# Graph network kernel: early banks at product tiles 10 to 31, five of six copied ahead, banks 17 and 23 copied by VectorE

## The reference, cut to what matters

```python
msg = x[src] + edge_attr                                # 206,250 edges of 128 numbers
agg = segment_sum(msg, dst, num_segments=6250)          # edges are sorted by dst
h = relu(agg @ W1 + b1) @ W2 + b2
# then a norm over everything, a norm per column, gelu, two residuals and a layer norm
```

## Time and profile before

| what | value |
|---|---|
| median of 3 runs | 779.25 us (778.49 to 780.11) |
| the profiled execution's own time | 778.32 us |
| its span, first to last instruction | 776.5 us |
| PE busy | 688.2 us, 89% |
| DVE busy | 619.9 us, 80% |
| ACT busy | 445.7 us, 57% |
| first product of chunk 0, of chunk 24 | 83.48 us, 667.46 us |

### The profile page before, as it was taken

How to read it: one execution, slowest core, us unless ns; L and a number is a source line. 1 busy time by engine, 2 the same in 40 slices (tenths; PEclk the granted TensorE clock), 3 DMA queues, 4 the chain that set the end, 5 groups by cost and what they waited for, 6 DMA issues and landing times.

```text
span 776.5 us, 25426 instructions
## 1 busy us (share of the span) xinstructions
PE 688.2 (89%) x9447; PEld 624.4 (80%) x9447; DVE 619.9 (80%) x1049; ACT 445.7 (57%) x993; POOL 101.2 (13%) x68
## 2 busy tenths in 40 slices
PE   1975999999999999999999999999999999989650
PEld 1954988998889988899888998889988899868530
DVE  5787898888988889888898888988888888435684
ACT  1934467655676556765567655676556765325475
POOL 2143110111101111011110112101111011000000
PEclk9986999999999999999999999999999999999965
DMA  7867466255662566525665256652565535350006
GB/s 175 288 215 218 138 208 198 64 189 195 205 194 67 185 199 203 187 75 180 204 202 172 92 176 209 196 183 87 176 209 191 178 97 176 106 160 6 0 0 165
DMA packets 88984, 123.60 MB, mean 159 GB/s; under 512 B 8572, under 2 KB 84446, under 8 KB 88763
## 3 DMA queue, kind: packets, MB, share of 16 engines
q1 hardware_dynamic: 82220, 116.30, 47.0%
q0 software_dynamic: 5744, 5.38, 2.6%
q10 hardware_dynamic: 1000, 1.65, 0.8%
HBM read 119.23 MB, written 4.03 MB: 159 GB/s over the span
## 4 chain that ended last, share of the span: by engine, by line
PE 65%; DVE 13%; issue 8%; ACT 6%; DVEq 4%; DMA 3%; ACTq 0%; SPq 0%; POOLq 0%
PE bank L792 39%; PE bank L758 10%; DVE pool_m L1079 8%; PE bank L709 5%; ACT counts L583 4%; PE bank L842 3%; PE bank L852 3%; PE bank L681 3%; DVEq L1006 2%; PE bank L723 1%; DMA edges<-in_edge_attr_dram 1%; DMA agg<-in_dst_dram 1%; ACT pool_m L665 1%; DVE onehot L990 1%; DMA begins<-listed,tile_slot 1%
## 5 line engine op out<-in xcount | busy, mean ns | idle before, releaser
L583 ACT CAST counts<-bank 128x490 fp32r<-128x490 f32 x625 | 329.3, 593 | 237.1 <-PE bank L758 222.8
L792 PE MATMUL bank<-counts,x_hi 128*128 128x250 f32 x1225 | 309.0, 291 | 12.1 <-ACT counts L583 12.1
L792 PE MATMUL bank<-counts,x_lo 128*128 128x250 f32 x1225 | 293.1, 279 | 0.0
L1079 DVE TENSOR_TENSOR pool_m<-value_row,turned_lo 128x3328 bf16<-128x3328 bf16 (+1 forms) x125 | 229.3, 1835 | 64.8 <-PE bank L758 64.6
L792 PEld LDWEIGHTS bank<-counts,x_hi 128*128 128x128 f32 x1225 | 231.2, 189 | 17.8 <-ACT counts L583 17.8
L792 PEld LDWEIGHTS bank<-counts,x_lo 128*128 128x128 f32 x1225 | 231.8, 189 | 0.0
L758 PE MATMUL bank<-pool_m 128*128 128x98 bf16 x3125 | 199.2, 211 | 15.6 <-DVE pool_m L1079 15.6
L758 PEld LDWEIGHTS bank<-pool_m 128*128 128x128 bf16 x3125 | 159.2, 99 | 37.1 <-issue 16.3
L1079 DVE TENSOR_TENSOR pool_m<-value_row,turned_key 128x2548 bf16<-128x2548 bf16 (+1 forms) x125 | 179.8, 1439 | 0.0
L709 PE MATMUL bank<-edges,onehot 128*32 128x128 f32 x3228 | 121.1, 284 | 4.5 <-DMA edges<-in_edge_attr_dram 3.7
L476 POOL DMA_INDIRECT near<-listed,row_slot x27 | 53.6, 1986 | 512.2 <-DVE row_slot L1041 469.6
(11 more groups left out here) (153 smaller groups left out, 420.5 us busy)
## 6 DMA issues: line engine op xcount, KB each, us to landing
edges<-in_edge_attr_dram SPq DMA_DIRECT2D x134, 768.0 KB, 8.2
out_dram<-pool_m SPq DMA_DIRECT2D x6, 512.0 KB
agg<-in_dst_dram SPq DMA_DIRECT2D x1, 768.0 KB
agg<-in_src_dram ACTq DMA_DIRECT2D x1, 768.0 KB
listed<-agg ACTq DMA_DIRECT2D x1, 768.0 KB
begins<-listed,tile_slot POOLq DMA_INDIRECT x28, 4.1
near<-listed,row_slot POOLq DMA_INDIRECT x27
pool_m<-in_L_gnn_W_dram SPq DMA_DIRECT2D x2, 128.0 KB, 2.8
```

The source lines that it names most:

```text
L583: nc.scalar.copy(counts[:, :, at:at + NODES], cps[k % RING][:, 0:NODES * NT].rearrange("p (n q) -> p q n", q=NT)).then_inc(banks_free, 1)
L792: last = nc.tensor.matmul(sps[:, 0:CHUNK], part[:, q, :], counts[:, q, at:at + CHUNK], start=(q == 0 and part is x_hi), stop=(q == NT - 1 ...
L1079: last = dve.tensor_tensor(to[b % MARKED][:, 0:wide[1]], values[:, :, 0:n, :].to_broadcast(wide), of.to_broadcast(wide), ALU.is_equal)
```

## The change

The six banks of the next chunk are still counted during the products, now under the name `COUNTED = 6`, but at tiles 10, 14, 18, 22, 26 and 31 in place of 22, 27, 32, 37, 42 and 47. Only five of them are copied during the products (`AHEAD = 5`, so 50 more columns in place of 60); the sixth stays in PSUM until `chunk_summed` and becomes the first copy of the counting phase. Of the 25 copies of each chunk, those of banks 17 and 23 move from ScalarE to VectorE (`keep_bank`, same source, destination and size), with a semaphore of their own, `banks_kept`, that TensorE waits for before it uses their ring places again and before the products. The VectorE order gets `keep_bank(c, 17)` behind `mark_batch(c, 4)`, and `keep_bank(c, 23)` ahead of `mark_batch(c + 1, 0)`.

```diff
-AHEAD = 6
-AHEAD_AT = (22, 27, 32, 37, 42, 47)
+AHEAD = 5
+COUNTED = 6
+COUNTED_AT = (10, 14, 18, 22, 26, 31)
+KEPT = (17, 23)
...
                 act.wait_ge(chunk_summed, c + 1)
                 for k in range(AHEAD, BANKS):
-                    copy_bank(c, k, odd)
+                    if k not in KEPT:
+                        copy_bank(c, k, odd)
...
                 if k >= RING:
-                    pe.wait_ge(banks_free, c * BANKS + (k + 1 - RING))
+                    if k - RING in KEPT:
+                        pe.wait_ge(banks_kept, c * len(KEPT) + (KEPT.index(k - RING) + 1))
+                    else:
+                        pe.wait_ge(banks_free, c * (BANKS - len(KEPT)) + (k + 1 - RING - sum(j < k - RING for j in KEPT)))
...
-                for k in range(AHEAD, BANKS):
+                for k in range(COUNTED, BANKS):
                     count_bank(c, k)
...
-                pe.wait_ge(banks_free, (c + 1) * BANKS)
+                pe.wait_ge(banks_free, (c + 1) * (BANKS - len(KEPT)))
+                pe.wait_ge(banks_kept, (c + 1) * len(KEPT))
...
-                    if q in AHEAD_AT and more:
-                        count_bank(c + 1, AHEAD_AT.index(q))
+                    if q in COUNTED_AT and more:
+                        count_bank(c + 1, COUNTED_AT.index(q))
...
+            def keep_bank(c, k):
+
+                dve.wait_ge(chunk_summed, c + 1)
+                dve.wait_ge(banks_done, c * BANKS + (k + 1 + CREDIT))
+                dve.tensor_copy(counts[:, :, k * NODES:(k + 1) * NODES],
+                                cps[k % RING][:, 0:NODES * NT].rearrange("p (n q) -> p q n", q=NT)
+                                ).then_inc(banks_kept, 1)
...
@@ -1138,6 +1154,7 @@
                 put(first)
                 mark_pair(p, 3)
                 mark_batch(c, 4)
+                keep_bank(c, KEPT[0])
                 if not last:
                     mark_pair(p, 4)
                     split_words(c + 2)
...
                     mark_pair(p, 5)
                     mark_pair(p, 6)
+                keep_bank(c, KEPT[-1])
+                if not last:
                     mark_batch(c + 1, 0)
...
                 mark_pair(p, 8)
                 mark_batch(c, 4)
+                keep_bank(c, KEPT[0])
                 add(first + 2, 0, base_of(first + 2), c + 1)
                 put(first + 3)
                 mark_pair(p, 9)
...
                 put(first + 4)
                 mark_pair(p + 1, 0)
+                keep_bank(c, KEPT[-1])
                 mark_batch(c + 1, 0)
```

More of the change, by code:

```diff
@@ L110, in gnn_kernel @@
     AHEAD_N = AHEAD * NODES
-    assert AHEAD * BANK <= EDGES_OF[2] and EDGES_OF[-1] == PAIRS + 1
+    assert AHEAD <= COUNTED and COUNTED * BANK <= EDGES_OF[2] and EDGES_OF[-1] == PAIRS + 1
     SPAN = 2 * P
@@ L292, in gnn_kernel @@
         banks_free = sem("banks_free")
+        banks_kept = sem("banks_kept")
         chunk_summed = sem("chunk_summed")
@@ L796, in _ @@
             pe.wait_ge(x_split, NT // PIECE)
-            for k in range(AHEAD):
+            for k in range(COUNTED):
                 count_bank(0, k)
```

## The result

The changed kernel takes 781.46 us (median of 8 runs, 780.27 to 783.73); the kernel before, measured again beside it, 778.96 us. The ratio is 1.0033, 95% interval 1.002 to 1.0046. It is 0.33% slower. The forecast was 774.3 us, with a range of 769.5 to 778.6 us and 0.76 on faster and 0.11 on slower; the time lies above the range.

What follows compares the result with a forecast made beforehand. TensorE was taken to bound the kernel, with reachable waits in each pair of chunks. Pairs gain 4.1 us and the last counting phase 0.8, together about 4.9 us, giving 774.3 us for a median, range 769.5 to 778.6 us.

Steps and rivals of the forecast that it cites:

- Part 1: ScalarE ends its counting-phase copies about 0.7 us sooner; first product about 10.15 us (odd), 10.25 us (even) after phase start.
- Part 2: Each bank copy on VectorE: a row of 0.667 us, costing the engine 0.58 us.
- B: Rival: the VectorE copy takes its engine more than 0.68 us; at 0.85 us the kernel takes 787 us; chance 0.11.
- C: Rival: the VectorE copy costs 0.667 us without overlap; 778.4 us, no change; chance 0.13 together with the rest of D.
- Part 3: VectorE's counting phase: after bank 17's copy and small operations, marks of batch 0 start 9.87 us (odd), 9.66 us (even) in.
- the register load: VectorE, odd chunks: loading the address `base_of`, some 0.65 us in all, fits behind bank 17's copy.
- Part 4: TensorE in the products: stands at tile 10 for the marks of batch 0, about 0.6 us (odd) and 0.5 us (even).
- 2.5 us of room: TensorE at tile 22 in the kernel before: some 2.5 us to spare there.
- The sum: Whole kernel: 11.5 pairs of chunks at 0.36 us give -4.1 us, last counting phase -0.8 us; about -4.9 us, 774.3 us.
- the old wait at bank 20: TensorE in odd counting phases of the kernel before: waits 0.19 us for marks of batch 4, which the change removes.
- D: Rival: ScalarE's last copy or VectorE's dispatch costs 0.1 to 0.2 us more a chunk; 0.07 still faster, rest within C's 0.13.

Runs made afterwards that it cites:

- run 1: Changed kernel with bank 17's VectorE copy moved behind add(first + 2) and put(first + 3) in odd chunks: 770.91 us, ratio 0.9898 to the kernel before.
- run 4: Changed kernel with early banks still at tiles 10 to 31, but all 25 copies on ScalarE: 777.0 us, ratio 0.9974 to the kernel before.
- run 8: Changed kernel with the first VectorE copy behind add and put in odd chunks, and bank 15 in place of 17: 769.9 us, ratio 0.9894.
- run 7: Changed kernel with bank 17's copy behind add and put in odd chunks, and early banks at tiles 14 to 34: 762.96 us, ratio 0.9801.
- run 2: Changed kernel with only the address load of add(first + 2) moved ahead of bank 17's copy in odd chunks: 776.6 us, ratio 0.9971.
- run 3: Changed kernel with the two VectorE copies kept, but early banks at tiles 22 to 47 and six copied ahead: 778.14 us, ratio 0.9998.
- run 6: Changed kernel with early banks at tiles 14 to 34 in place of 10 to 31, VectorE order kept: 773.15 us, ratio 0.9924.

## Why the prediction was wrong

**Part 1, ScalarE's end and the first product.** The numbers are right: in even chunks C' + 10.25, measured 278.15 - 267.90 = 10.25. In odd chunks the same number was hidden by the missed wait, and appeared when that was removed (run 1: 10.14 for 10.15). The hit is in part luck. ScalarE's last copies in the changed kernel:

```profile
276.76 1.15 ACT L586 CAST counts<-bank 128x490 fp32r<-128x490 f32 x2
```

They end at 277.91, C' + 10.01, where before they ended at C' + 10.84: 0.83 us sooner, and not 0.7. But the first product now starts 0.24 us behind them, and before it started 0.05 us behind (251.77 + 1.99 = 253.76, product at 253.81). I had no term for that step of 0.19 us. In the changed kernel it is there in 24 of the 25 chunks and absent in the last, whose code stands behind the loop; in run 4, without the copies on VectorE and without TensorE's wait for `banks_kept`, it is absent in all. VectorE's own last copy is not what is late: in run 8 it ends 1.19 us ahead of the product (273.53, 274.72), and the product still starts 0.24 us behind ScalarE (274.48). What is left is the wait for `banks_kept`, one wait more between the one for ScalarE's copies and the first product in TensorE's queue (`chunk_added` stands there in both kernels); no run has moved that wait by itself, so this cause is argued. In the changed kernel the stall at tile 10 hides the step. In run 7 nothing does, and 24 times 0.19 us is an estimate of 4.6 us at most that is still to be had there.

**Part 2, the price of the copy.** Right. 0.66 to 0.67 us a row, 0.667 forecast; the next instruction starts 0.58 us after the copy's start (253.03 to 253.61), 0.58 forecast. Rivals B and C fall with this. By the drain rule of the Trainium skill ("VectorE: DVE Perf Modes", section "The DRAIN you can't avoid") the slot would have been the whole 0.66 us. The same section makes an exception, which the forecast left out: a next instruction that is not held starts earlier. The 0.58 us of this trace go with the exception and not with the rule.

**Part 3, the small operations behind bank 17.** This is the step that failed: "The operations ahead of it are done at about 6.82 + 1.33 = 8.15". I followed VectorE's queue to VectorE's own next wait, the turn at bank 20, and found room. I did not ask who on another engine waits for the operations in between. The first of them is `add(first + 2)`. The edge half at bank 20 begins a group and waits for it (`edges_added` in `begin_half`), because it reuses the PSUM bank that the add reads. Before, this add was done just in time. The half started 0.55 us after the add's start (249.67 to 250.22); where it has to wait for the add, it starts 0.51 to 0.53 us after it (runs 2 and 3, and the changed kernel). So there were some 0.03 us to spare, and no row of waits showed it. With the wait for bank 17, the copy and the load put ahead of it, it ended at C + 7.5, TensorE's half came at C + 7.77 (250.73 - 242.96) where without the wait it comes at C + 6.83 (run 1, 248.54 - 241.71), and the turn that I took as C + 7.78 came at 251.52, C + 8.56.

The term was mis-sized as well: "the register load [...] fits behind the copy". The load starts only when the wait for bank 17 has let the queue go (249.29), and the add follows 0.91 us later, not 0.65, so it stuck out by 0.33 us behind the copy. Run 2 puts this part at about half of the wait.

**Part 4, the stall at tile 10.** Right. The even bank 0 came at C' + 13.11 (281.01 - 267.90), 13.07 forecast, and the 8 us that run 6 wins are this stall. Its size, start to start, is about 0.4 us in both kinds of chunk, where 0.5 and 0.6 were forecast; the bracket shows 0.26 of it. The "2.5 us of room" at tile 22 before was 3.35 us in odd chunks (marks at 252.52 and 3.41 us more make 255.93, and bank 0 ran at 259.28); nothing hung on it. The distance from bank 0 to the next counting phase, 10.98 us forecast, is 242.96 - 232.03 = 10.93.

**The sum.** The odd cycle was wrong by 24.94 - 24.26 = 0.68 us; 12 odd chunks make 8.2 us, and 774.3 + 8.2 = 782.5, with 781.46 measured. Of the 1 us between them, 0.4 is the last counting phase, which took 669.26 - 659.64 = 9.62 us, 1.2 us less than before where I had said 0.8, and 0.3 is the kernel before, now 778.96 us for 779.25; the rest is open. The 0.68 us are two errors that partly cancel. The missed wait costs 0.93 us in an odd chunk (24.94 against 24.01 in run 1), and the ledger without it was 0.25 us too long, mostly because it took the old wait at bank 20 as 0.19 us and not 0.37.

**The rivals.** None was right. D had the right place in its words ("VectorE's dispatch behind the wait for bank 17") and a price of 0.1 to 0.2 us; it was 0.68 in every second chunk. The rival on the slow side was a price for the copy, the one term that rows had pinned down best. B and C were also priced too high: they count the price four times a pair, but by the forecast's own ledger the first copy of an odd chunk has 0.25 us to spare (8.15 against 8.40), so C's 0.087 us count three times, 0.26 of the 0.36 us.

## What to carry to other kernels

When a wait and its instruction are put into an in-order queue, list every semaphore that the instructions behind it raise, and look up for each the other engines' waits in the code, not in the table of waits: a wait that is met with 0.03 us to spare has no row until something moves. What a wait costs is read from start to start; the idle time in a bracket gave 0.19 us here for a wait that cost 0.37. Put the new wait behind the instruction that another engine needs next, and address loads ahead of it. And try two repairs together: against the kernel before, the change with the new order won 1.0%, with later tiles 0.8%, with both 2.0%.

## What the runs showed of the hardware

A copy of 128x490 f32 from PSUM with a turned read into f32r takes VectorE 665 ns, on average of 50:

```profile
L1095 DVE CAST counts<-bank 128x490 fp32r<-128x490 f32 x50 | 33.2, 665 | 22.9 <-PE bank L765 22.9
```

On ScalarE the same copy is 604 ns in this kernel (575 of them). The VectorE copy of the earlier trace rows, 128x408 in 582 ns, also turns the order and writes short runs (of six elements, here ten); the 82 more elements cost 83 ns. What the turned read and the short runs cost by themselves no run separates.

The address that VectorE loads into a register cost nothing where the queue was not held in front of it (the add 0.60 us behind the copy in run 3, 0.59 with the load moved ahead in run 2). It cost 0.41 us where the queue had just been released from a wait (0.99 us in the changed kernel, of which 0.33 show as idle).

In the loop, with TensorE's wait for `banks_kept` between its waits for `banks_free` and `chunk_added`, the first product starts 0.24 us behind ScalarE's last copy (the changed kernel, runs 1, 3, 7 and 8, wherever it waits for that copy); without that wait it is 0.05 us (the kernel before, run 4). That the added wait is the cause is argued and not tested.
